# Scores of two heads in one visit every fourth step, in front of the seventh product, with the blocks of two heads kept

## Time and profile before

| what | value |
|---|---|
| median of 3 runs | 1465.92 us (1465.64, 1465.92, 1467.06) |
| profiled execution, span of its instructions | 1464.0 us |
| instructions | 37072 |
| TensorE busy | 1459.2 us |
| VectorE, ScalarE, GpSimd busy | 1089.7, 726.7, 752.5 us |
| granted TensorE clock | 1.000 |

### The profile page before, as it was taken

One profiled execution on the slowest core, in us unless ns is written; L12 is line 12 of the kernel. 1 busy time (PEld: TensorE's weight loads), 2 busy tenths in 40 slices (PEclk: granted clock), 3 DMA queues, 4 the chain that ended last, 5 costly groups with the idle time before them and its releaser, 6 DMA issues.

```text
span 1464.0 us, 37072 instructions
## 1 busy us (share of the span) xinstructions
PE 1459.2 (100%) x15683; PEld 1262.6 (86%) x15683; DVE 1089.7 (74%) x1505; ACT 726.7 (50%) x1330; POOL 752.5 (51%) x532
## 2 busy tenths in 40 slices
PE   9999999999999999999999999999999999999999
PEld 8788888888888888888999999999888888888887
DVE  8787868788786877874498889988677676667663
ACT  7767677666767667675333333344443222222221
POOL 7667777787777877775444444454453112112100
PEclk9999999999999999999999999999999999999999
DMA  4211111110111101111433433447474244244230
GB/s 151 66 44 45 38 36 38 45 45 31 37 45 45 44 24 44 45 44 59 153 129 131 143 128 133 137 155 228 151 233 131 83 135 131 74 136 140 73 116 30
DMA packets 106998, 135.28 MB, mean 92 GB/s; under 512 B 6224, under 2 KB 89424, under 8 KB 106320
## 3 DMA queue, kind: packets, MB, share of 16 engines
q1 hardware_dynamic: 105968, 132.49, 27.4%
q10 hardware_dynamic: 864, 0.42, 0.1%
HBM read 86.75 MB, written 46.14 MB: 91 GB/s over the span
## 4 chain that ended last, share of the span: by engine, by line
PE 96%; DVE 2%; ACT 1%; issue 1%; DVEq 0%; POOL 0%; ACTq 0%; POOLq 0%
PE bank L672 39%; PE bank L906 24%; PE bank L683 22%; PE bank L865 4%; PE bank L791 3%; PE bank L934 1%; PE bank L952 1%; PE bank L621 0%; DVE qreg L1654 0%; DVE wa L1548 0%; PE bank L600 0%; DVE xs_lo L1611 0%; DVE qreg L1633 0%; PE bank L963 0%; PE bank L920 0%
## 5 line engine op out<-in xcount | busy, mean ns | idle before, releaser
L672 PE MATMUL bank<-xs_hi,wa 128*128 128x512 f32 x1792 | 563.4, 392 | 0.2
L1454 POOL TENSOR_TENSOR accr<-accr,sqst 128x512 f32<-128x512 f32 x248 | 352.8, 1433 | 148.1 <-ACT sqst L1136 108.4
L672 PEld LDWEIGHTS bank<-xs_hi,wa 128*128 128x128 f32 x1792 | 336.3, 188 | 74.3 <-DVE qk L1700 2.4
L672 PE MATMUL bank<-xs_lo,wa 128*128 128x512 f32 x896 | 348.6, 389 | 0.0
L683 PE MATMUL bank<-wv,xs_hi 128*128 128x256 f32 x1792 | 323.3, 283 | 0.1
L906 PE MATMUL bank<-ot,wo_main 128*128 128x512 f32 x1344 | 316.6, 392 | 0.0
L906 PEld LDWEIGHTS bank<-ot,wo_main 128*128 128x128 f32 x1344 | 249.5, 188 | 52.6
L683 PEld LDWEIGHTS bank<-wv,xs_hi 128*128 128x128 f32 x1792 | 279.6, 192 | 2.2 <-issue 1.9
L683 PE MATMUL bank<-wv,xs_lo 128*128 128x256 f32 x896 | 253.5, 283 | 0.0
L1548 DVE TENSOR_TENSOR wa<-wraw,wa 128x256 fp32r<-128x256 f32 (+1 forms) x160 | 157.5, 985 | 96.5 <-ACT wa L1052 94.7
L1261 ACT ACTIVATE ot<-bank,vec 128x256 fp32r<-128x256 f32 x256 | 100.3, 476 | 239.4 <-PE bank L906 146.4
(11 more groups left out here) (222 smaller groups left out, 1729.3 us busy)
## 6 DMA issues: line engine op xcount, KB each, us to landing
values_b<-v_spill SPq DMA_DIRECT2D x62, 512.0 KB, 4.8
wraw<-in_wqk SPq DMA_DIRECT2D x32, 512.0 KB, 3.6
v_spill<-vo SPq DMA_DIRECT2D x64, 256.0 KB, 2.3
v_spill<-sqst SPq DMA_DIRECT2D x64, 256.0 KB, 2.3
score_spill<-sqst SPq DMA_DIRECT2D x32, 256.0 KB, 2.0
wraw<-in_wv SPq DMA_DIRECT2D x16, 512.0 KB, 5.1
wraw<-score_spill SPq DMA_DIRECT2D x16, 512.0 KB, 4.1
accr<-in_wo SPq DMA_DIRECT2D x16, 512.0 KB, 5.9
```

The costliest lines, as they stand in the source:

```text
L672: ins = pe.matmul(dst[:, :], wa[:, col:col + P], xpart[:, j - 1, kt, n * CH:(n + 1) * CH], start=(first and k == 0), stop=(k == 5), skip_g ...
L1454: pool.tensor_tensor(a, a, sq_slot(count), ALU.add).then_inc(acc_done, 1)
```

## The change

`scores` is called in steps `s % 4 == 0` from step 4 on, for two heads (`s // 2 - 2` and `s // 2 - 1`), one product earlier than before: in front of `p7(s)`. The last two heads are done together behind `p6(64)`. So that the blocks of two heads can wait, each of `q_hi`, `k_lo`, `k_hi` has 4 slots and `q_lo` 5, in `qk`, a new tensor `qk_more` (128 x 4096 float32) and `sqst`. The copies (`keep_scores`) are done in steps `s % 4 == 0` (first head) and `s % 4 == 1` (second head), each followed by its spill on SyncE; the last one moves behind `block_22(64)`. `block_22` waits for the scores only in steps `s % 4 == 0`, and for the first of the two heads. The wait of the lora product for `kept` is gone, and the scratch for dynamic DMAs is set to 64.

```diff
+        qk_more = sb("qk_more", [P, 4096])
...
-        blk = {(name, par): qk[:, (2 * i + par) * 512:(2 * i + par + 1) * 512]
-               for i, name in enumerate(("q_lo", "q_hi", "k_lo", "k_hi")) for par in range(2)}
-        blk["q_lo", 2] = sqst[:, 3, :]
+        SLOTS = {"q_lo": 5, "q_hi": 4, "k_lo": 4, "k_hi": 4}
+        blk = {}
+        for i, name in enumerate(SLOTS):
+            for par in range(4):
+                blk[name, par] = (qk_more, qk)[par // 2][:, (2 * i + par % 2) * 512:(2 * i + par % 2 + 1) * 512]
+        blk["q_lo", 3], blk["q_lo", 4] = sqst[:, 3, :], blk["q_lo", 3]
...
-                if s % 2 == 0:
-                    sp.wait_ge(kept, s // 2)
-                    sp.dma_start(spill[s // 2 - 1], stage).then_inc(spilled, 16)
-
-            sp.wait_ge(kept, H)
-            sp.dma_start(spill[H - 1], stage).then_inc(spilled, 16)
+                if s >= 4 and s % 4 < 2:
+                    h = s // 4 * 2 - 2 + s % 4
+                    sp.wait_ge(kept, h + 1)
+                    sp.dma_start(spill[h], stage).then_inc(spilled, 16)
+
+            sp.wait_ge(kept, H - 1)
+            sp.dma_start(spill[H - 2], stage).then_inc(spilled, 16)
...
+                if s == N_QK:
+                    sp.wait_ge(kept, H)
+                    sp.dma_start(spill[H - 1], stage).then_inc(spilled, 16)
...
-                if h == 1:
+                if h == 0:
                     pe.wait_ge(lora_used, 2)
...
                 p1(s + 1)
+                if s % 4 == 0:
+                    scores(s // 2 - 2)
+                    scores(s // 2 - 1)
                 p7(s)
-                if s % 2 == 0:
-                    scores(s // 2 - 1)
                 p2(s + 1)
                 if s == 3:
-                    pe.wait_ge(kept, 1)
                     lora(0)
...
             p6(N_QK)
+            scores(H - 2)
             scores(H - 1)
...
-                    act.wait_ge(scored, H - 1)
+                    act.wait_ge(scored, H - 2)
...
-                    dst = blk["q_lo", s % 3]
-                    if s == 2:
+                    dst = blk["q_lo", s % 5]
+                    if s == 3:
                         dve.wait_ge(t_lo, t_at(2, 7))
...
-                    dst = blk["k_hi", s % 2]
-                    if s % 2 == 0:
-                        dve.wait_ge(scored, s // 2)
+                    dst = blk["k_hi", s % 4]
+                    if s % 4 == 0 and s >= 4:
+                        dve.wait_ge(scored, s // 2 - 1)
...
-                if s % 2 == 0 and s >= 2:
-                    keep_scores(s // 2 - 1)
+                if s >= 4 and s % 4 < 2:
+                    keep_scores(s // 4 * 2 - 2 + s % 4)
...
-            keep_scores(H - 1)
+            keep_scores(H - 2)
...
                 block_22(s)
+                if s == N_QK:
+                    keep_scores(H - 1)
...
-    nc = bacc.Bacc("TRN2", target_bir_lowering=False, num_devices=1)
+    nc = bacc.Bacc("TRN2", target_bir_lowering=False, num_devices=1, dynamic_dma_scratch_size=64)
```

More of the change, by code:

```diff
@@ L785, in scores @@
                     s, part = 2 * h + n % 2, ("lo", "hi")[n // 2]
-                    q, k = blk["q_" + part, s % (3 if part == "lo" else 2)], blk["k_" + part, s % 2]
+                    q, k = blk["q_" + part, s % SLOTS["q_" + part]], blk["k_" + part, s % 4]
                     for t in range(TC):
@@ L1140, in gain @@
             def gain(name, s, ready):
-                q = blk[name, s % (3 if name == "q_lo" else 2)]
+                q = blk[name, s % SLOTS[name]]
                 act.activation(q, q, ACT.Copy, scale=vec[:, s // 2, 3:4]).then_inc(ready, 1)
@@ L1146, in last_q @@
                 act.wait_ge(c12_done, s + 1)
-                square(sq_q_hi(s), 0, s % 2 + 2, blk["q_hi", s % 2], None)
+                square(sq_q_hi(s), 0, s % 2 + 2, blk["q_hi", s % 4], None)
             x_block(0, 0)
@@ L1197, in _ @@
                 act.wait_ge(c11_done, s + 1)
-                square(sq_q_lo(s), 0, s % 2, blk["q_lo", s % 3], None)
+                square(sq_q_lo(s), 0, s % 2, blk["q_lo", s % 5], None)
                 gain("q_lo", s, gq_lo)
@@ L1219, in _ @@
                 act.wait_ge(c22_done, s + 1)
-                square(sq_k_hi(s), 1, s % 2 + 2, blk["k_hi", s % 2], None)
+                square(sq_k_hi(s), 1, s % 2 + 2, blk["k_hi", s % 4], None)
                 if s % 2 == 0 and s >= 2 and h + 1 < H:
@@ L1223, in _ @@
                 act.wait_ge(p_done[4], s + 1)
-                act.activation(blk["k_lo", s % 2], bank_a(s)[:, :], ACT.Identity, bias=vec[:, h, 1:2], scale=1.0)\
+                act.activation(blk["k_lo", s % 4], bank_a(s)[:, :], ACT.Identity, bias=vec[:, h, 1:2], scale=1.0)\
                    .then_inc(c21_done, 1)
@@ L1705, in block_12 @@
                 if s < N_QK:
-                    dst = blk["q_hi", s % 2]
+                    dst = blk["q_hi", s % 4]
                 else:
```

## The result

The changed kernel takes **1512.70 us** (four runs, 1508.76 to 1513.90) against 1466.18 us for the kernel before: 1.0312 times as long, with a 95% interval from 1.0298 to 1.0327. Slower was forecast, 46.5 us weren't: the forecast was +5.4 us and the range ended at 1475.5. The profiled execution is the 1508.76 us one.

A forecast was written before the change was run, and what follows sets the result against it. TensorE, busy 1459.2 of 1464.0 us, was taken as the bound. The terms -5.1 + 7.0 + 1.7 + 0.9 + 0.9 gave +5.4 us, so 1471.3 us, with a range from 1463.5 to 1475.5 us.

The forecast's parts named there:

- What a second head costs inside a visit: Between a visit's two heads: five waits might cost nothing or a full 0.32 us; nothing was taken.
- The prediction's own sign of being wrong: In visits: a gap between the two heads in every visit was listed among the signs of a wrong forecast.
- The ways in and out: Entering and leaving score visits on TensorE: 16 fewer visits at 0.32 us each save 5.1 us.
- Steps 14, 26, 38, 50: Steps losing their visit after a two-level step: TensorE idles 1.86 us in each at p3, net 7.0 us.
- The shift: Delay reaching p3 from the added keep_scores copy in odd steps: between 0 and 0.60 us, taken as 0.3.
- Steps 2 and 6: p3 waits for VectorE's k_hi block: net 0.9 us in step 2 and 1.7 us in step 6.
- Late q_hi: Visits moved ahead of p7 in steps 8, 20, 32, 44, 56: second head waits for q_hi, net 0.9 us.
- The vector engine found no time: Rival, steps 24 to 26: VectorE frees over 1.56 us, so p3 finds k_hi ready; 1461.9 us, chance 0.14.
- neither did half of it: Rival, same mechanism or a3 and k_hi slightly earlier: stalls of about 0.8 us; 1466 us, no change, chance 0.17.
- The third, a second price in the visit: Rival, between heads: drain paid per head, waits cost the same 0.32 us each, nothing saved; 1476.4 us, chance 0.06.

The follow-up runs named there:

- The pair of runs with half of the scores: The kernel before and the changed kernel, each with half of every head's score matmuls left out: 1455.51 us and 1459.62 us.
- the waits moved: The changed kernel with half of the score matmuls left out, and both heads' waits put in front of the first head: 1465.02 us.
- the doubled one: The kernel before, with every visit computing its one head's scores twice into the same bank: 1585.59 us, ratio 1.0784.
- one product between: The changed kernel with the two heads of a step on both sides of p7(s), the last pair still together: 1486.55 us, ratio 1.0135.
- the burst of one and a half times: The kernel before, with every visit computing its head and then its first half again, 192 score matmuls instead of 128: 1523.07 us, ratio 1.0383.

## Why the prediction was wrong

**The step that failed** is "What a second head costs inside a visit is not in the trace of L791 ... Bounds: nothing, or a full 0.32 ... I take nothing". Both bounds were too low. It asked only what the waits between the heads can cost and never what 512 instructions in 2.2 us need from the instruction stream. The second head cost 2 us at its block end in each visit (31.4 us), 0.155 us for its waits (2.4 us, also not nothing), 0.5 us more in the visits of steps 24, 36, 48 and 60 (gaps of 0.27 to 0.31 us, each 0.35 us behind a block end; why they are longer wasn't tested), and the clock behind some of the stops (2.2 us in the profiled execution, more in the others). The row that I leaned on, 31 "issue" stops for 64 calls of L865, could show neither: its pairs are 128 matmuls in 1.9 us, with half the block ends, and the trace has no wait instruction between the two calls of a pair (the second starts 0.038 us after the first, a distance that is common in that burst), where between two heads it has one or two. The prediction's own sign of being wrong, a gap between the two heads in every visit, came out in all 16.

**What held, point by point.**
- The ways in and out: 32 visits became 16 and saved 5.1 us, 0.32 each, as computed.
- **Steps 14, 26, 38, 50:** 1.86 us forecast, 1.53 to 1.55 measured in each, and the order as argued: first `keep_a3`, then VectorE. Step 26 after, in the timelines of TensorE and VectorE:

```profile
317.11 0.39 PE L680 MATMUL bank<-xs_hi,wa 128*128 128x512 f32 x1
317.91 0.50 PE L680 MATMUL bank<-xs_hi,wa 128*128 128x512 f32 x1 [0.41 <-ACT snap L1133]
...
319.55 1.10 PE L680 MATMUL bank<-xs_hi,wa 128*128 128x512 f32 x2 [0.21 <-DVE wa L1557]
```

```profile
306.15 1.11 DVE L1557 TENSOR_TENSOR wa<-wraw,wa 128x512 fp32r<-128x512 f32 x1 [1.84 <-ACT wa L1061]
...
308.06 0.68 DVE L1681 COPY sqst<-bank 128x512 f32<-128x512 f32 x1
...
309.59 1.18 DVE L1662 TENSOR_SCALAR qreg<-qreg,thr,step 128x1024 f32<-128x1024 f32 x1
...
319.42 0.68 DVE L1709 TENSOR_TENSOR qk<-bank,snap 128x512 f32<-128x512 f32 x1
```

  From the key split to the end of k_hi it is 320.10 - 306.15 = 13.95 us, and before it was 301.49 - 287.54 = 13.95: the added copy reached p3 with nothing. The level behind it took 1.18 us instead of 1.73, since it began 0.6 us later beside the same GpSimd instruction and, counted from the key split, ended at nearly the same place (4.62 us, and 4.57 before). The shift was 0, the lower bound, and 1.56 us the right number. The exclusive lock of the Trainium skill (SBUF — State Buffer, section "SBUF: two separate sides") had pointed that way, and these times agree with it. A part of the idle time is a wait for p3's weights (L1557, key 3), which stands ahead of p4's last matmul and which I hadn't named.
- **Steps 2 and 6:** 0.72 us against 0.93 forecast, 2.46 against 2.05. Between them 0.8 us were lost that I had at nothing (0.39 at 63 us, 0.42 at 83 us).
- **Late q_hi** in steps 8, 20, 32, 44, 56: gaps of 0.54 to 0.58 us between the heads, 0.4 above the plain one, against 0.27 forecast for step 20 and 0.56 for step 8. It came to 2.0 us above the plain gap, where the forecast had 1.6 before it took off 0.7 for what those steps lost in the kernel before.
- Taken together: without the stops and the clock the balance has +9.2 us. Without the 2.4 and 0.5 us of gaps that the forecast had at nothing it has +6.3, where the forecast was +5.4. The pair of runs with half of the scores, in which the stops are out of play, has 4.1.
- **The rivals.** The vector engine found no time, and neither did half of it. The third, a second price in the visit, had the right place and the wrong price: 0.155 us a visit for waits, where it had 0.32, and nothing for a drain (0.015 with the waits moved).

What stays open: why a fetch begins 0.65 us after a block end in one visit and 1.55 in another, and now and then several us late; why TensorE goes on only 1.2 us or more after the packet has landed; and what of the 4 us between the 1508.76 us execution and the slowest is the clock alone.

## What to carry to other kernels

Count instructions, not only microseconds, before merging bursts of tiny matmuls: here TensorE's program comes in blocks of 256 (128 weight load and matmul pairs), the fetch for a block end inside a burst takes 3 to 4 us from the block end before it, and a block of 128x32 score matmuls is run through in 1.1 us, so a burst with two block ends in it pays more for the fetch (2 us) than a merged visit saves (0.32 us). Put several us of large matmuls between such bursts: with three products, 4.1 us, between the heads 14 of 15 steps ran without a stop. And when a visit is taken out of a step, read what the other engines have at its end: the visit had been cover for them, and a step whose vector work fills it gives the time back.

## What the hardware showed that I had not expected

- A block end that TensorE reaches too early stops it until 1.20 to 1.61 us after the packet of the block end before has landed. Where that earlier end lies in the scores too, this is 2.95 to 3.85 us after it: in the changed kernel, in the doubled one (3.1 to 3.85), and with one product between (3.14 to 3.71). Where it lay at the scores' very start, the packet was out 0.2 to 0.8 us before TensorE came to it, and the stop ended 1.7 to 2.2 us after it (five visits of the burst of one and a half times).
- The stops have a second price: behind some of them the granted clock is at the lower level (0.51 in the window above), and the doubled kernel spent 10.6 us more in its products for it.
- The group of five semaphore waits between two heads, all met, costs 0.155 us in the middle of a burst of 9 ns starts, and such groups cost nothing visible between products of 227 ns.
- A change of bank and of operands inside the burst costs nothing (0.015 us against 0.009).
